# Eight-core two-layer block on Trainium2: two diagonal tiles and a later evacuation wait in the layer-0 convolution, one activation tile instead of two in the layer-1 QKV projection

## The chip, the cores and the metric

The kernel runs on the 8 cores of one Trainium2 chip, two dies of four cores. Every core runs the same program on its own batch element (2048 tokens of 1024 features). The time is device microseconds of the slowest core, from launch to end; lower is better. TensorE (PE) does matmuls, VectorE (DVE) and ScalarE (ACT) do elementwise work, GpSimd (POOL) issues the weight loads, and SyncE (SP) issues the other DMAs.

## The reference, cut to what matters

Two layers. Each is `x = x + s * g` with `s` an attention-like branch and `g` a silu-gated feed-forward branch on the layernormed input. The change touches one step of each layer's attention branch.

```
# layer 0: projection, causal depthwise convolution over 4 taps, then value and gate
z = x @ W_in
z = conv_general_dilated(z, w_conv, padding=[(CONV_K - 1, 0)], feature_group_count=...) + b_conv
x_val = z[..., :D]                  # 1024 channels
x_gate = silu(z[..., D:2 * D])      # 1024 channels
...                                 # decayed running sums, norm, W_out
# layer 1: projection to q, k, v
qkv = hidden_states @ Wqkv.T + bqkv
...                                 # rope, windowed attention, full attention, Wd
```

Layer 0's feed-forward works on fake-quantized operands; layer 1's is a mixture of 8 experts (MoE).

## The kernel before, in words

**Layer 0 attention** (`emit_l0_attn`) walks over 4 chunks `tc` of 512 tokens. In each chunk the first stage is the projection with the convolution, 16 feature blocks `fc`:

- POOL loads the block's weights (`wfc`, 256 KB) into one of two buffers, after the projection that used this buffer two blocks before.
- PE runs 8 matmuls of 512 columns into PSUM (L769).
- DVE copies 3 old columns (L773), casts the PSUM bank to the bf16 tile `zr` (L775), keeps the last 3 columns (L778), then builds four 128x128 diagonal matrices from the identity and the tap weights into the one tile `diag4` (L783), and signals with a small memset (L787).
- PE runs 4 matmuls, one for each tap, with the diagonals as stationary operand (L795).
- ACT evacuates that bank into `xv` (L799) or, with silu, into `gate` (L803).
- PE waits for ACT, and DVE for PE, before the next block.

After the 16 blocks comes DVE's scan for the denominator and its reciprocal (L827, L837), the main stage of the chunk, the output projection (L1053, with weight loads of the same size, L1044), and the residual (L1085). PE runs the first projection of the next chunk already during the residual.

**Layer 1 QKV** (`emit_l1_attn`) walks over 4 chunks `tt` of 512 tokens. It has 32 output blocks `oc` in each: POOL loads 256 KB of weights (`wstq`, two buffers, L1676), PE runs 8 matmuls (L1686), and ACT evacuates with the bias (L1702, L1711). For the last 8 blocks SP transposes the result (L1721). The chunk's activations, `xnb_q` (1 MB), lie in two buffers. The load of chunk `tt + 1` is issued on SP at the start of chunk `tt`, behind the transposes of chunk `tt - 1` (L1663).

Of the kernel before, what the change touches and what calls it, by code (L numbers as in the profile page):

```python
# [7 lines left out]
BF16 = mybir.dt.bfloat16  # L8
U32 = mybir.dt.uint32
AF = mybir.ActivationFunctionType  # L10
ALU = mybir.AluOpType
# [18 lines left out]
class KB:  # L30
# [75 lines left out]
    def wait(self, eng, sem, val):  # L106
        assert val <= self.cnt(sem), (sem, val, self.cnt(sem))
        self.q[eng].append(
            lambda E, _s=sem, _v=val: E[eng].wait_ge(E["S"][_s], _v))
# [549 lines left out]
def emit_l0_attn(kb, pb, want_dbg=False):  # L659
    H, op, wait, drain = kb.H, kb.op, kb.wait, kb.drain  # L660
    sb = kb.sb
# [4 lines left out]
    smalls = sb["smalls"]  # L666
# [8 lines left out]
    wre = kb.S("wre", (128, 32), F32)  # L675
    wim = kb.S("wim", (128, 32), F32)
    wy = kb.S("wy", (128, 8 * 128), BF16)
    diag4 = kb.S("diag4", (128, 4 * 128), BF16)
    zr = [kb.S(f"zr{i}", (128, TC + 3), BF16) for i in range(2)]
    ztail = kb.S("ztail", (128, 16 * 3), BF16)  # L680
    xv = kb.S("xv", (128, 8 * TC), F32)
# [69 lines left out]
    for tc in range(NTC):  # L751
        t0 = tc * TC
        first = tc == 0
        for fc in range(16):
            bz = fc % 2
            in_ap = bass.AP(H["l0_win2"].tensor, fc * 131072,
                            [[1024, 128], [1, 1024]])
            if wfc_guard[bz]:
                kb.wait("gpsimd", "te", wfc_guard[bz])
            lw = op("gpsimd", lambda e, _i=in_ap, _b=bz: e.dma_start(  # L760
                out=wfc[_b][:], in_=_i), "gw", 16)
            wait("tensor", "gw", lw)
            bank = pb[2 + bz]
            mmv = None
            for dc in range(8):
                mov = xn_fm[:, dc * T + t0:dc * T + t0 + TC]
                sta = wfc[bz][:, dc * 128:(dc + 1) * 128]
                mmv = op("tensor", lambda e, _b=bank, _s=sta, _m=mov, _d=dc:
                         e.matmul(_b[:], _s, _m, start=(_d == 0), stop=(_d == 7)),  # L769
                         "te" if dc == 7 else None)  # L770
            wfc_guard[bz] = mmv
            wait("vector", "te", mmv)
            op("vector", lambda e, _b=bz, _f=fc: e.tensor_copy(  # L773
                zr[_b][:, 0:3], ztail[:, _f * 3:_f * 3 + 3]))
            ev = op("vector", lambda e, _b=bank, _z=bz: e.tensor_copy(  # L775
                zr[_z][:, 3:3 + TC], _b[:]), "dve")
            kb.drain("vector")
            op("vector", lambda e, _b=bz, _f=fc: e.tensor_copy(  # L778
                ztail[:, _f * 3:_f * 3 + 3], zr[_b][:, TC:TC + 3]))
            wait("tensor", "dve", ev)  # L780
            wait("vector", "te", wfc_guard[bz])
            for tap in range(4):
                op("vector", lambda e, _f=fc, _t=tap: e.tensor_scalar(  # L783
                    out=diag4[:, _t * 128:(_t + 1) * 128], in0=sb["ident"][:],
                    scalar1=wconv[:, (_f * 4 + _t):(_f * 4 + _t) + 1],
                    scalar2=None, op0=ALU.mult))
            v_diag = op("vector", lambda e: e.memset(smalls[:, 3:4], 0.0), "dve")  # L787
            wait("tensor", "dve", v_diag)
            bank2 = pb[4 + bz]
            mmv2 = None  # L790
            for tap in range(4):
                mov = zr[bz][:, tap:tap + TC]
                sta = diag4[:, tap * 128:(tap + 1) * 128]
                mmv2 = op("tensor", lambda e, _b=bank2, _s=sta, _m=mov, _t=tap:
                          e.matmul(_b[:], _s, _m, start=(_t == 0), stop=(_t == 3)),  # L795
                          "te" if tap == 3 else None)
            wait("scalar", "te", mmv2)
            if fc < 8:
                a = op("scalar", lambda e, _b=bank2, _f=fc: e.activation(  # L799
                    xv[:, _f * TC:(_f + 1) * TC], _b[:], AF.Identity,  # L800
                    bias=bconv[:, _f:_f + 1], scale=1.0), "act")
            else:
                a = op("scalar", lambda e, _b=bank2, _f=fc: e.activation(  # L803
                    gate[:, (_f - 8) * TC:(_f - 7) * TC], _b[:], AF.Silu,
                    bias=bconv[:, _f:_f + 1], scale=1.0), "act")
            wait("tensor", "act", a)
            wait("vector", "te", mmv2)
        a_convdone = kb.cnt("act")

        if want_dbg and "dbg_xv" in H:  # L810
# [812 lines left out]
def emit_l1_attn(kb, want_dbg=False):  # L1623
# [13 lines left out]
    ones1b = sb["ones1b"]  # L1637
    relub, ubuf = sb["relub"], sb["ubuf"]
    M_R = kb.marker()
    xnb2 = [kb.S(f"xnb_q{i}", (128, 8 * 512), BF16) for i in range(2)]  # L1640
    wst = [kb.S(f"wstq{i}", (128, 8 * 128), BF16) for i in range(2)]
    rot = kb.S("rot", (128, 128), BF16)
    cosl = kb.S("cosl", (128, 512), BF16)
# [5 lines left out]
    wst_guard = [0, 0]  # L1649
    evac_hist = []  # L1650
    vtp_hist = []
    mm_tt = [0, 0]
    lx_t = {0: op("sync", lambda e: e.dma_start(
        out=xnb2[0][:], in_=bass.AP(H["xn1"].tensor, 0,
                                    [[2048, 128], [128 * 2048, 8], [1, 512]])),
        "ld", 16)}
    for tt in range(4):
        xnb = xnb2[tt % 2]
        if tt + 1 < 4:
            if mm_tt[(tt + 1) % 2]:  # L1660
                wait("sync", "te", mm_tt[(tt + 1) % 2])
            lx_t[tt + 1] = op("sync", lambda e, _t=tt + 1,
                              _o=xnb2[(tt + 1) % 2]: e.dma_start(  # L1663
                out=_o[:],
                in_=bass.AP(H["xn1"].tensor, _t * 512,
                            [[2048, 128], [128 * 2048, 8], [1, 512]])),
                "ld", 16)
        lx = lx_t[tt]
        wait("tensor", "ld", lx)
        for oc in range(32):  # L1670
            bws = oc % 2
            if wst_guard[bws]:
                kb.wait("gpsimd", "te", wst_guard[bws])
            in_w = bass.AP(H["l1_wqkvT"].tensor, oc * 131072,
                           [[1024, 128], [1, 1024]])
            lww = op("gpsimd", lambda e, _i=in_w, _b=bws: e.dma_start(  # L1676
                out=wst[_b][:], in_=_i), "gw", 16)
            wait("tensor", "gw", lww)
            if len(evac_hist) >= 4:
                wait("tensor", "act", evac_hist[-4])  # L1680
            bank = pb[oc % 4]
            mmv = None
            for dc in range(8):
                mmv = op("tensor", lambda e, _b=bank, _s=wst[bws][:, dc * 128:(dc + 1) * 128],
                         _m=xnb[:, dc * 512:(dc + 1) * 512], _d=dc:
                         e.matmul(_b, _s, _m, start=(_d == 0), stop=(_d == 7)),  # L1686
                         "te" if dc == 7 else None)
            wst_guard[bws] = mmv
            mm_tt[tt % 2] = mmv
            wait("scalar", "te", mmv)  # L1690
            if oc < 4:
                dst = qsl[:, oc * T + tt * 512:oc * T + tt * 512 + 512]
            elif oc < 8:
                dst = ksl[:, (oc - 4) * T + tt * 512:(oc - 4) * T + tt * 512 + 512]
            elif oc < 16:
                dst = qrest[:, (oc - 8) * T + tt * 512:(oc - 8) * T + tt * 512 + 512]
            elif oc < 24:
                dst = krest[:, (oc - 16) * T + tt * 512:(oc - 16) * T + tt * 512 + 512]
            else:
                dst = v_tm[:, (oc - 24) * T + tt * 512:(oc - 24) * T + tt * 512 + 512]  # L1700
            if oc < 24:
                a_e = op("scalar", lambda e, _b=bank, _d=dst, _o=oc: e.activation(  # L1702
                    _d, _b, AF.Identity, bias=sb["bqkv_t"][:, _o:_o + 1],
                    scale=1.0), "act")
                evac_hist.append(a_e)
            else:
                vstage = sb["relub"] if (oc % 2 == 0) else sb["ubuf"]
                if len(vtp_hist) >= 2:
                    wait("scalar", "tp", vtp_hist[-2])
                a_e = op("scalar", lambda e, _b=bank, _o=oc, _v=vstage:  # L1710
                         e.activation(_v[:], _b, AF.Identity,  # L1711
                                      bias=sb["bqkv_t"][:, _o:_o + 1],
                                      scale=1.0), "act")
                evac_hist.append(a_e)
                wait("sync", "act", a_e)
                pair = oc - 24
                sa = vstage[:].rearrange("p (i q) -> p i q", q=128)
                da = bass.AP(v_tm, pair * T + tt * 512,
                             [[8 * T, 128], [128, 4], [1, 128]])
                tpv = op("sync", lambda e, _s=sa, _d=da:  # L1720
                         e.dma_start_transpose(_d, _s), "tp", 16)  # L1721
                vtp_hist.append(tpv)
# [556 lines left out]
```

How the kernel before makes its waits and increments, by code:

```python
    def op(self, eng, f, inc=None, n=1):  # L89
        if inc is None:
            self.q[eng].append(lambda E, _f=f: _f(E[eng]))
            return None
        if n == 16:
            prev = self.counts.get(inc, 0)
            if prev:
                self.wait(eng, inc, prev)
        self.counts[inc] = self.counts.get(inc, 0) + n
        v = self.counts[inc]
        self.q[eng].append(
            lambda E, _f=f, _s=inc, _n=n: _f(E[eng]).then_inc(E["S"][_s], _n))
        return v
# [4 lines left out]
    def wait(self, eng, sem, val):  # L106
        assert val <= self.cnt(sem), (sem, val, self.cnt(sem))
        self.q[eng].append(
            lambda E, _s=sem, _v=val: E[eng].wait_ge(E["S"][_s], _v))
```

## Time and profile before

| | us |
|---|---|
| median of 3 runs | 6670.56 (6667.47 to 6677.14) |
| profiled execution, its own time | 6681.63 |
| its span, core 0, the slowest | 6680.3 |
| spans of the 8 cores | 6645.3 to 6680.3 |
| PE, DVE, ACT, POOL busy on core 0 | 2580.4, 2019.9, 1265.4, 189.0 |
| mean granted TensorE clock of the cores | 0.636 to 0.639 |

A time beside a line is the engine's busy time in that group. "Idle before" is how long the engine stood still just ahead of the group, with what released it. The releaser is inferred from semaphore events: where an instruction waits for several semaphores the view names only one. The granted clock is a share of 2.4 GHz: 512 columns take 0.213 us at 2.4 GHz and 0.427 us at 1.2 GHz. The time outside the span is 1.3 us.

### The profile page before, as it was taken

To read this page: it belongs to the slowest core of one execution; us is meant where nothing else is said; L and a number is where in the kernel's file an instruction comes from. 1 tells how busy PE (TensorE), PEld (TensorE's weight loads), DVE (VectorE), ACT (ScalarE), POOL (GpSimd) and SP (SyncE) were. 2 spreads that over 40 slices of the span, in tenths; PEclk is the share of its full clock that TensorE was granted. 3 is DMA by queue.
4 is the path that set the end of the run, shared out by engine and by line. 5 is a ranking of instruction groups with operands and counts; after the bars stand their busy time and mean duration, and the time that the engine had idled before them with its cause. 6 is when DMAs were issued, how large, how long until landed. Compare 5 with 4: busy or idle time off the path is not lost.

```text
span 6680.3 us, 35761 instructions; the slowest of 8 cores (6645.3 to 6680.3 us)
## 1 busy us (share of the span) xinstructions
PE 2580.4 (39%) x8358; PEld 826.1 (12%) x8358; DVE 2019.9 (30%) x4521; ACT 1265.4 (19%) x2230; POOL 189.0 (3%) x358
## 2 busy tenths in 40 slices
PE   0005422422423422105444555534444655555531
PEld 0002100100100100002111211101111311111110
DVE  8882463364365166121110000021222011111121
ACT  0001120110111021001110111104333244444300
POOL 0000000000000000000000011100000000000000
PEclk9997555655555555558777877755555855555576
DMA  2211102101200200434555444420000300000024
GB/s 51 47 42 15 18 0 46 23 0 27 42 0 12 56 2 1 91 67 77 72 82 76 85 66 68 62 33 1 1 1 1 51 2 5 5 5 5 8 51 134
DMA packets 271576, 239.39 MB, mean 36 GB/s; under 512 B 191826, under 2 KB 213970, under 8 KB 271346
## 3 DMA queue, kind: packets, MB, share of 16 engines
q0 software_dynamic: 52768, 116.50, 12.1%
q1 hardware_dynamic: 218610, 120.60, 8.8%
q8 instruction: 81, 1.33, 0.1%
q14 instruction: 117, 0.96, 0.1%
HBM read 284.17 MB, written 25.17 MB: 46 GB/s over the span
## 4 chain that ended last, share of the span: by engine, by line
DMA 30%; DVE 24%; PE 24%; ACT 10%; issue 9%; DVEq 2%; SPq 0%; ACTq 0%; POOLq 0%
DMA wstq<-l_wqkvT 8%; PE PS L2106 4%; ACT ptcol L2086 3%; PE PS L769 3%; DMA maskb<-masksf 3%; DVE csre L925 2%; DVE csim L928 2%; PE PS L2075 2%; DMA wst<-l_wd 2%; ACT ptw L1879 2%; DMA wgu<-l_wg 2%; DMA wgu<-l_wu 2%; PE PS L1999 2%; DMA wfc<-l_win 2%; DMA wfc<-l_wout 1%
## 5 line engine op out<-in xcount | busy, mean ns | idle before, releaser
L1686 PE MATMUL PS<-xnb_q,wstq 128*128 128x512 bf16 x1024 | 344.0, 497 | 281.8 <-DMA wstq<-l_wqkvT 255.7
L2086 ACT ACTIVATE ptcol<-PS,negmb 128x512 bf16<-128x512 f32 (+3 forms) x640 | 357.5, 623 | 469.0 <-PE PS L2075 468.9
L947 PE MATMUL PS<-rein,psum 128*32 128x512 bf16 x128 | 76.4, 597 | 869.8 <-DVE imin L941 869.8
L1551 PE MATMUL PS<-xnb,wgu 128*128 128x512 bf16 x1024 | 260.5, 420 | 321.2 <-DMA xnb<-xn 235.5
L2106 PE MATMUL PS<-ptcol,a 128*65 128x512 bf16 (+3 forms) x640 | 281.2, 556 | 237.6 <-ACT ptcol L2086 128.8
L2075 PE MATMUL PS<-xn_fm,g 64*128 64x512 bf16 (+3 forms) x640 | 277.1, 555 | 127.8 <-DMA A_fm<-outsb 127.3
L769 PE MATMUL PS<-xn_fm,wfc 128*128 128x512 bf16 x512 | 219.7, 606 | 97.8 <-DMA wfc<-l_win 61.1
L549 PE MATMUL PS<-xq_fm,wqT 128*128 128x512 bf16 x256 | 57.1, 387 | 495.5 <-DMA wqT<-wq_st 495.5
L891 ACT ACTIVATE sinb<-frac 128x512 bf16<-128x512 f32 x128 | 73.0, 617 | 874.9 <-DVE frac L884 874.9
L1742 DVE TENSOR_TENSOR qsl<-qsl,cosl 128x512 bf16<-128x512 bf16 x16 | 6.8, 426 | 716.8 <-DMA g<-ubuf 682.6
L1568 DVE TENSOR_TENSOR relub<-relub 128x512 bf16<-128x512 bf16 x64 | 27.2, 426 | 648.4 <-ACT ubuf L1563 648.4
L795 PE MATMUL PS<-zr,diag 128*128 128x512 bf16 x256 | 90.3, 489 | 271.1 <-DVE smalls L787 271.1
L1895 PE MATMUL PS<-g,ptw 128*128 128x64 bf16 x256 | 54.4, 212 | 340.2 <-DVE ptw L1884 340.2
L1686 PEld LDWEIGHTS PS<-xnb_q,wstq 128*128 128x128 bf16 x1024 | 110.9, 116 | 514.5 <-issue 466.0
L1597 PE MATMUL PS<-inter,wst 128*128 128x512 bf16 x512 | 140.5, 437 | 87.0 <-DMA wst<-l_wd 51.2
L2092 DVE TENSOR_TENSOR ptcol<-ptcol,cmask 128x128 bf16<-128x128 bf16 x256 | 57.7, 225 | 365.8 <-ACT ptcol L2086 365.8
L1551 PEld LDWEIGHTS PS<-xnb,wgu 128*128 128x128 bf16 x1024 | 106.5, 106 | 474.8 <-issue 380.6
L925 DVE TENSOR_TENSOR_SCAN csre<-rein,carr 128x512 bf16<-128x512 bf16 x128 | 162.6, 1271 | 7.0 <-DVE imin L919 0.5
L2063 DVE COPY a<-A_tm 128x64 bf16<-128x64 bf16 x256 | 46.1, 180 | 391.2 <-PE PS L2106 391.2
L928 DVE TENSOR_TENSOR_SCAN csim<-imin,carr 128x512 bf16<-128x512 bf16 x128 | 161.0, 1258 | 0.0
L1884 DVE TENSOR_TENSOR ptw<-ptw,wmask 128x256 bf16<-128x256 bf16 (+1 forms) x256 | 73.8, 288 | 263.4 <-ACT ptw L1879 263.4
L1920 ACT ACTIVATE A_tm<-PS,rdc 128x64 bf16<-128x64 f32 x256 | 80.4, 314 | 364.9 <-DVE rdc L1914 364.9
(268 smaller groups left out, 4194.5 us busy)
## 6 DMA issues: line engine op xcount, KB each, us to landing
wstq<-l_wqkvT POOLq DMA_DIRECT2D x128, 256.0 KB, 4.1
wfc<-l_win POOLq DMA_DIRECT2D x64, 256.0 KB, 3.9
wgu<-l_wg POOLq DMA_DIRECT2D x32, 512.0 KB, 5.2
wgu<-l_wu POOLq DMA_DIRECT2D x32, 512.0 KB, 5.2
wst<-l_wd POOLq DMA_DIRECT2D x32, 512.0 KB, 5.6
xt<-x SPq DMA_DIRECT2D x16, 512.0 KB
wfc<-l_wout POOLq DMA_DIRECT2D x32, 256.0 KB, 3.9
xt_l<-x SPq DMA_DIRECT2D x16, 512.0 KB
```

Source lines behind the costliest of these rows:

```text
L769: e.matmul(_b[:], _s, _m, start=(_d == 0), stop=(_d == 7)),
L795: e.matmul(_b[:], _s, _m, start=(_t == 0), stop=(_t == 3)),
L925: op("vector", lambda e, _ci=ci, _p=p: e.tensor_tensor_scan(csre[_p][:], rein[_p][:], rein[_p][:], carr[:, _ci:_ci + 1], ALU.add, ALU.bypass))
L928: g = op("vector", lambda e, _ci=ci, _p=p: e.tensor_tensor_scan(csim[_p][:], imin[_p][:], imin[_p][:], carr[:, _ci + 1:_ci + 2], ALU.add, ...
L1551: _h=hc: e.matmul(_b, _s, _m, start=(_h == 0), stop=(_h == 7)),
L1597: e.matmul(_b, _s, _m, start=(_k == 0), stop=(_k == 15)),
L1686: e.matmul(_b, _s, _m, start=(_d == 0), stop=(_d == 7)),
L1879: e.activation(ptw[_b][:, 0:_n], _S[:, 0:_n], AF.Exp, bias=negmb1[:, _h:_h + 1], scale=0.125),
L1999: _d=dc: e.matmul(_b, _s, _m, start=(_d == 0), stop=(_d == 7)),
L2075: _w=w, _r=half * 64: e.matmul(PS[:, _o:_o + _w], _k, _q, start=True, stop=True, tile_position=(_r, 0)), "te")
L2086: e.activation(ptcol[:, _o:_o + _w], PS[:, _o:_o + _w], AF.Exp, bias=negmb2[:, _h:_h + 1], scale=0.125), "act")
L2106: e.matmul(PS[0:65, OB0 + _q * 128:OB0 + _q * 128 + _w], a65[_b][:, 0:65], _p, start=_st, stop=_sp), "te")
```

## The change

It has two parts, in two stages that lie some 1500 us apart.

In the convolution `diag4` becomes two tiles. The diagonals of block `fc + 1` are built on DVE right after the copies of block `fc`, the first ones at the head of the chunk. The small memset is gone. PE no longer waits for ACT after each block. Its tap matmuls wait for the evacuation two blocks before, which used the same PSUM bank, and one wait for all evacuations stands behind the 16 blocks. DVE's wait for the tap matmuls is gone.

In the QKV projection the two tiles for the activations become one. The load of a chunk is issued at the chunk's head, when all matmuls before it are done.

```diff
-    diag4 = kb.S("diag4", (128, 4 * 128), BF16)
+    diag4 = [kb.S(f"diag4_{i}", (128, 4 * 128), BF16) for i in range(2)]
...
+        def build_diag(fcx):
+            for tap in range(4):
+                g = op("vector", lambda e, _f=fcx, _t=tap, _d=diag4[fcx % 2]:
+                       e.tensor_scalar(
+                    out=_d[:, _t * 128:(_t + 1) * 128], in0=sb["ident"][:],
+                    scalar1=wconv[:, (_f * 4 + _t):(_f * 4 + _t) + 1],
+                    scalar2=None, op0=ALU.mult), "dve" if tap == 3 else None)
+            return g
+
+        wait("vector", "te", kb.cnt("te"))
+        diag_v = {0: build_diag(0)}
+        act_hist = []
...
+            if fc + 1 < 16:
+                diag_v[fc + 1] = build_diag(fc + 1)
             wait("tensor", "dve", ev)
-            wait("vector", "te", wfc_guard[bz])
-            for tap in range(4):
-                op("vector", lambda e, _f=fc, _t=tap: e.tensor_scalar(
...
-            v_diag = op("vector", lambda e: e.memset(smalls[:, 3:4], 0.0), "dve")
-            wait("tensor", "dve", v_diag)
+            wait("tensor", "dve", diag_v[fc])
+            if len(act_hist) >= 2:
+                wait("tensor", "act", act_hist[-2])
...
-            wait("tensor", "act", a)
-            wait("vector", "te", mmv2)
+            act_hist.append(a)
+        wait("tensor", "act", kb.cnt("act"))
...
-    xnb2 = [kb.S(f"xnb_q{i}", (128, 8 * 512), BF16) for i in range(2)]
+    xnb = kb.S("xnb_q", (128, 8 * 512), BF16)
...
-            lx_t[tt + 1] = op("sync", lambda e, _t=tt + 1,
-                              _o=xnb2[(tt + 1) % 2]: e.dma_start(
...
+        wait("sync", "te", kb.cnt("te"))
+        lx = op("sync", lambda e, _t=tt: e.dma_start(
+            out=xnb[:], in_=bass.AP(H["xn1"].tensor, _t * 512,
                                     [[2048, 128], [128 * 2048, 8], [1, 512]])),
-        "ld", 16)}
```

PE, the first blocks of a chunk, before. PS is PSUM, `wfc` the projection weights, `diag` the diagonals.

```order
L769 MATMUL PS<-xn_fm,wfc 128x512 [waits act,gw]
L769 MATMUL PS<-xn_fm,wfc 128x512 x7
L795 MATMUL PS<-zr,diag 128x512 [waits dve]
L795 MATMUL PS<-zr,diag 128x512 x3
L769 MATMUL PS<-xn_fm,wfc 128x512 [waits act,gw]
L769 MATMUL PS<-xn_fm,wfc 128x512 x7
```

The same place now (L781 is the projection, L804 the taps).

```order
L781 MATMUL PS<-xn_fm,wfc 128x512 [waits gw]
L781 MATMUL PS<-xn_fm,wfc 128x512 x7
L804 MATMUL PS<-zr,diag_0 128x512 [waits dve,act]
L804 MATMUL PS<-zr,diag_0 128x512 x3
L781 MATMUL PS<-xn_fm,wfc 128x512 [waits gw]
L781 MATMUL PS<-xn_fm,wfc 128x512 x7
L804 MATMUL PS<-zr,diag_1 128x512 [waits dve,act]
```

The order of the matmuls is the same. The wait for ACT has moved from the projection to the taps, where it asks for an evacuation two blocks old.

DVE in the same blocks, before.

```order
L773 COPY zr<-ztail 128x3 [waits te]
L775 CAST zr<-PS 128x512
L778 COPY ztail<-zr 128x3
L783 TENSOR_SCALAR diag<-ident,wconv 128x128 [waits te]
L783 TENSOR_SCALAR diag<-ident,wconv 128x128 x3
L787 MEMSET smalls 128x1
```

And now (L757 builds diagonals, L787 is now the cast).

```order
L757 TENSOR_SCALAR diag_1<-ident,wconv 128x128 x4
L785 COPY zr<-ztail 128x3 [waits te]
L787 CAST zr<-PS 128x512
L790 COPY ztail<-zr 128x3
L757 TENSOR_SCALAR diag_0<-ident,wconv 128x128 x4
```

The diagonals that the taps of a block read now stand ahead of that block's copies.

SP in the QKV stage from its first instruction, before. `xnb_q` is the activation tile, `g` the transposed values.

```order
L1653 DMA xnb_q<-xn 128x8x512 [waits ld]
L1663 DMA xnb_q<-xn 128x8x512 [waits ld]
L1721 DMA_TRANSPOSE g<-relub 128x4x128 [waits act,tp]
...
L1721 DMA_TRANSPOSE g<-ubuf 128x4x128 [waits act,tp]
L1663 DMA xnb_q<-xn 128x8x512 [waits te,ld]
```

And now.

```order
L1663 DMA xnb_q<-xn 128x8x512 [waits te,ld]
L1718 DMA_TRANSPOSE g<-relub 128x4x128 [waits act,tp]
...
L1718 DMA_TRANSPOSE g<-ubuf 128x4x128 [waits act,tp]
L1663 DMA xnb_q<-xn 128x8x512 [waits te,ld]
```

One of the two loads at the head is gone. The load that stands behind the eight transposes of a chunk used to bring the chunk after next, and now brings the next one.

## Rows read from the trace of the kernel before

**Rows 1.** Costliest groups: line, engine, operation; busy us, mean ns; idle before, releaser.
```profile
L769 PE MATMUL PS<-xn_fm,wfc 128*128 128x512 bf16 x512 | 219.7, 606 | 97.8 <-DMA wfc<-l_win 61.1
```

**Rows 2.** Timeline of one block, first chunk: start, us, engine, line; idle before, releaser.
```profile
641.53 3.57 PE L769 MATMUL PS<-xn_fm,wfc 128*128 128x512 bf16 x8 [1.03 <-ACT xv L799]
...
645.29 0.69 DVE L775 CAST zr<-PS 128x512 bf16<-128x512 f32 x1
...
646.17 0.84 DVE L783 TENSOR_SCALAR diag<-ident,wconv 128x128 bf16<-128x128 bf16 x4
646.96 0.06 DVE L787 MEMSET smalls<- 128x1 f32 x1
...
647.17 1.02 PE L795 MATMUL PS<-zr,diag 128*128 128x512 bf16 x4 [2.06 <-DVE smalls L787]
648.29 0.69 ACT L799 ACTIVATE xv<-PS,bconv 128x512 f32<-128x512 f32 x1 [7.01 <-PE PS L795]
...
649.23 3.46 PE L769 MATMUL PS<-xn_fm,wfc 128*128 128x512 bf16 x8 [1.03 <-DMA wfc<-l_win]
```

**Rows 3.** Timeline of POOL, third and fourth weight load of the first chunk.
```profile
616.00 0.53 POOL L760 DMA_DIRECT2D wfc<-l_win  x1 [3.87 <-DMA wfc<-l_win]
637.28 0.53 POOL L760 DMA_DIRECT2D wfc<-l_win  x1 [20.74 <-PE PS L769]
```

**Rows 4.** Chain of waits, first tap matmuls of the second and third chunk.
```profile
1159.71 1.88 PE PS L795 x4
...
1688.02 1.88 PE PS L795 x4
```

**Rows 5.** Timeline, last tap matmuls of the second and third chunk.
```profile
1278.56 1.02 PE L795 MATMUL PS<-zr,diag 128*128 128x512 bf16 x4 [1.96 <-DVE smalls L787]
...
1809.39 1.87 PE L795 MATMUL PS<-zr,diag 128*128 128x512 bf16 x4 [1.96 <-DVE smalls L787]
```

**Rows 6.** Timeline of POOL in the first output projection, first load and the seventh.
```profile
1079.68 0.53 POOL L1044 DMA_DIRECT2D wfc<-l_wout  x1 [330.37 <-PE PS L1053]
...
1106.76 0.53 POOL L760 DMA_DIRECT2D wfc<-l_win  x1 [3.87 <-DMA wfc<-l_wout]
```

**Rows 7.** Windows: stretch, us, busy by engine (instructions), granted clock, DMA share, GB/s.
```profile
630.00:751.00 121.00, 73.97 (x184) 21.20 (x184) 24.40 (x122) 11.59 (x16) 7.96 (x15) 0.64 0.23 32
3795.00:4408.00 613.00, 344.10 (x1025) 111.00 (x1025) 0.00 (x0) 87.97 (x128) 67.44 (x127) 0.77 0.47 66
...
6430.00:6540.00 110.00, 60.36 (x242) 22.16 (x243) 12.75 (x30) 20.61 (x30) 3.18 (x6) 0.95 0.25 54
```

**Rows 8.** Timeline, one group of the last projection, 8 matmuls.
```profile
6449.94 1.89 PE L2201 MATMUL PS<-A_tm,wstd 128*128 128x512 bf16 x8 [1.63 <-DVE xn_fm L2219]
```

**Rows 9.** Chain of waits, behind the convolution of the second chunk.
```profile
1279.69 1.27 DVE l L827
```

**Rows 10.** Chain of waits at the start of the QKV stage.
```profile
3786.24 8.38 DMA xnb_q<-xn
3794.62 0.39 issue
```

**Rows 11.** Timeline of SP at the second and third border between QKV chunks.
```profile
4104.16 0.48 SPq L1663 DMA_DIRECT2D xnb_q<-xn  x1
...
4254.95 1.19 SPq L1721 DMA_TRANSPOSE g<-ubuf  x1
```

**Rows 12.** Chain of waits at the same borders, weight loads.
```profile
4104.48 8.16 DMA wstq<-l_wqkvT
...
4113.17 3.96 DMA wstq<-l_wqkvT
...
4262.39 3.82 DMA wstq<-l_wqkvT
```

**Rows 13.** Costliest groups, MoE.
```profile
L1551 PE MATMUL PS<-xnb,wgu 128*128 128x512 bf16 x1024 | 260.5, 420 | 321.2 <-DMA xnb<-xn 235.5
```

**Rows 14.** Chain of waits, the MoE load of the same tensor.
```profile
3232.47 6.70 DMA xnb<-xn
```

More of the change, by code:

```diff
@@ L779, in emit_l0_attn @@
                 ztail[:, _f * 3:_f * 3 + 3], zr[_b][:, TC:TC + 3]))
+            if fc + 1 < 16:
+                diag_v[fc + 1] = build_diag(fc + 1)
             wait("tensor", "dve", ev)
-            wait("vector", "te", wfc_guard[bz])
-            for tap in range(4):
-                op("vector", lambda e, _f=fc, _t=tap: e.tensor_scalar(
-                    out=diag4[:, _t * 128:(_t + 1) * 128], in0=sb["ident"][:],
-                    scalar1=wconv[:, (_f * 4 + _t):(_f * 4 + _t) + 1],
-                    scalar2=None, op0=ALU.mult))
-            v_diag = op("vector", lambda e: e.memset(smalls[:, 3:4], 0.0), "dve")
-            wait("tensor", "dve", v_diag)
+            wait("tensor", "dve", diag_v[fc])
+            if len(act_hist) >= 2:
+                wait("tensor", "act", act_hist[-2])
             bank2 = pb[4 + bz]
@@ L792, in emit_l0_attn @@
                 mov = zr[bz][:, tap:tap + TC]
-                sta = diag4[:, tap * 128:(tap + 1) * 128]
+                sta = diag4[fc % 2][:, tap * 128:(tap + 1) * 128]
                 mmv2 = op("tensor", lambda e, _b=bank2, _s=sta, _m=mov, _t=tap:
@@ L1651, in emit_l1_attn @@
     vtp_hist = []
-    mm_tt = [0, 0]
-    lx_t = {0: op("sync", lambda e: e.dma_start(
-        out=xnb2[0][:], in_=bass.AP(H["xn1"].tensor, 0,
+    for tt in range(4):
+        wait("sync", "te", kb.cnt("te"))
+        lx = op("sync", lambda e, _t=tt: e.dma_start(
+            out=xnb[:], in_=bass.AP(H["xn1"].tensor, _t * 512,
                                     [[2048, 128], [128 * 2048, 8], [1, 512]])),
-        "ld", 16)}
[L1657 to L1661, printed above, removed]
-            lx_t[tt + 1] = op("sync", lambda e, _t=tt + 1,
-                              _o=xnb2[(tt + 1) % 2]: e.dma_start(
[L1664 to L1668, printed above, removed]
+            "ld", 16)
         wait("tensor", "ld", lx)
@@ L1688, in emit_l1_attn @@
             wst_guard[bws] = mmv
-            mm_tt[tt % 2] = mmv
             wait("scalar", "te", mmv)
```

## The prediction

> **What bounds the kernel now.** I read the page's groups first. In the layer-0 projection PE stands idle 97.8 us ahead of its 512 matmuls, most of it put down to the weight DMA [rows 1]. That would mean that the convolution stage is bound by its loads, so I checked it in the timeline of one block [rows 2]. The reader is to see a closed ring there: projection on PE from 641.53 for 3.57, DVE's cast, four diagonals, the memset, the taps on PE at 647.17, ACT's evacuation at 648.29, and only then the next projection at 649.23. No two engines work side by side. The view names the DMA as what released 649.23. But the load that this fourth block needs is the fourth one, issued at 637.28 [rows 3], 12 us earlier, and the load before it had POOL waiting only 3.87 us for its predecessor. ACT ended at 648.29 + 0.69 = 648.98, and PE began 0.25 us later. So the ring is the bound, and the DMA in that row is the wrong name: the order lists show two waits there, for act and gw.
>
> How long the ring takes: the second chunk runs from its first taps at 1159.71 [rows 4] to its last at 1278.56 [rows 5], 118.85 us for 15 blocks, 7.92 each; the third from 1688.02 to 1809.39, 121.37 us, 8.09 each. The first and fourth lie between them. Four chunks at the mean of the two are 480.4 us, for 60 block periods of 8.01.
>
> The QKV stage is another case: at its borders POOL's weight loads follow one another in the chain of waits [rows 12], and PE waits for them. PE time there is not on the path; what shifts the weight loads is.
>
> **Part one, the convolution: what goes.** Three pieces leave the ring.
> - The diagonals and the memset. The taps begin when the cast is done, 645.29 + 0.69 = 645.98, plus the 0.15 us that the signal took from the memset's end, 647.02, to 647.17: 646.13 instead of 647.17, 1.04 us less. The four diagonals (0.84 us, the same four instructions as before) now run on DVE beside the taps and the next projection. All of DVE's work for a block, from the cast's start to the memset's end, is 647.02 - 645.29 = 1.7 us, against a period over 4: covered. Without cover it would be the 1.04 again.
> - The evacuation. The projection used to begin 2.06 us after the taps' start; now it follows four matmuls of 0.213 us, 0.85 us after it at the high clock: 1.2 us less. The new wait of the taps for the evacuation two blocks back asks for something a whole period old. Behind it stand only the taps and the next projection.
> - DVE's wait for the taps, which only matters at a chunk's end (below).
>
> **What is late next.** Two things can be. PE alone: projection 1.89 us at 2.4 GHz [rows 8] or 3.57 at 1.2 [rows 2], then 1.03 from its end to the taps (0.88 for the cast, 0.15 for the signal), then 0.85 for the taps, or 1.71 at 1.2 GHz. That is 3.77 us with all at the high clock, 5.45 with the projection alone at the low one, 6.31 with both. And the weight chain: POOL keeps one 256 KB load in flight. The output projection has loads of the same size, back to back: from 1079.68 to 1106.76 [rows 6], 27.08 us for 6, 4.51 each. So the period cannot fall much under 4.5 even when PE could do it in 3.77.
>
> Which clock? The stage was granted 0.64 with PE in ring waits half the time [rows 7]. In the last projection PE works 1.89 us and waits 1.63 [rows 8], and is granted 0.95. In QKV there are 128 groups of 8 matmuls in 613 us, 4.8 each with 2.7 of PE, and it is granted 0.77. The new pattern has 12 matmuls, 2.6 us, in 4.5, with the waits split in two: more work in a period than in the last projection (8 matmuls, 1.7 us, in 3.5). I take mostly the high clock, hence the weight chain as the bound, with about one period in ten at 5.45: 4.6 us. Bounds: 4.4 from below (the load at 616.00 came after 3.87 us of waiting for the one before it and POOL's own 0.53 [rows 3]), 6.31 from above.
>
> The sum: 480.4 - 60 x 4.6 = 204.4 us.
>
> **The chunk's ends.** DVE's scan started 1279.69 - 1278.56 = 1.13 us after the last taps began [rows 5, 9], and stands in the chain. It now starts behind the last cast and copy, about when the taps begin: 1 us less, 2 where the taps are slow, 4 times: 5. At a chunk's head the first diagonals stand ahead of the cast instead of behind it, the same work; the memset's step is worth nothing. DVE's new wait there is for PE work that it needed anyway. I put the ends at 5 us, between 2 and 8. Together part one gives 209.
>
> **Part two, the QKV projection: what comes.** At the first chunk nothing changes for PE: its load took 8.38 us and 0.39 to start [rows 10]. At three borders the load is now in the open. It is issued where the load for the chunk after next stood in SP's list, so at the second border at 4104.16, at the third after the last transpose, 4254.95 + 1.19 = 4256.2 with the queue's steps [rows 11]. It has one weight load beside it, like the first one, so 8.38 and 0.39: PE starts at 4112.9 and 4265.0. POOL's next weight load must wait for that group's end, at the low clock 3.57 later, and 0.6 for POOL: 4117.1 and 4269.2. Before, these loads were issued at 4113.17 and 4262.39 [rows 12]. The second border costs 3.9, the third 6.8. The second is cheap because the early load had its own price there: the weight load beside it took 8.16 us where its neighbour took 3.96. The first border had one too; I price it at the mean, 5.4. Part two costs 3 x 5.4 = 16 us. From below 11: with 6.70 us for the load, as in MoE [rows 14], each border is 1.7 cheaper. From above 26: 8.77 us at each of three, nothing given back.
>
> The Trainium skill (DMA: Bandwidth & Descriptors, Rules for kernel authors) says to issue a DMA early and wait for it late, which speaks against this part. By it alone the whole 8.77 us of each border is lost, 26 us, and the sum would be 10 us worse. Here the trace agrees in sign only.
>
> Net: 6681.63 - 209 + 16 = 6488.6 for the profiled execution. That one lay 11.07 above the median of 6670.56, so the median to expect is 6477.5; I say 6477.
>
> **Rivals.**
> - *A, the low clock stays.* PE splits its work by two waits in every period and is granted no more than now. Then the period is 5.45 rather than 4.6: 51 us less gain, 6528; at 6.31 it is 6580. For it: the stage had only 0.64, and QKV with waits of similar length 0.77 [rows 7]. Against it: the last projection at 0.95. The Trainium skill (TensorE: Matmul & The Clock Gate, A second HAM failure mode: psum-queue depth-cycling) describes this case: short idle spells between groups of matmuls that cycle through PSUM banks make the clock swing between its two levels. By it the time would be rival A's; the row of the last projection does not agree, the row of QKV does.
> - *B, the change does not open the ring.* If the row that names the DMA at 649.23 were right [rows 2], the next projection would need a load that is issued only after the last one, and the period would lose little: 0.4 us at most over 60 blocks, 24, less the 16 of part two, 6663. Against it: the count of loads above.
> - *C, slower.* The exposed load behaves like that in MoE, where PE waited 235.5 us over four chunks for the chunk's data, 58.9 each [rows 13]. There are no mask loads ahead of it here. Its place is each of three borders, and it decides from (209 + 13) / 3 = 74 us a border, where the time is 13 us above the present one. At 80 us a border it is 6702. At MoE's own 58.9 it would still be 6638.
>
> **How the numbers follow.** The forecast 0.64, with its own range: periods of 4.4 to 4.9 and part two from 11 to 26 give 6460 to 6505. Rival A 0.29, between 6505 and 6580. B 0.04, within 0.2% of the present time, which is 13 us and about what a measurement of this kernel can tell from no change. C 0.03. The range takes in most of A, and 20 us under the forecast's own low end, since all loads here that I could time stood beside other work: 6440 to 6560. Faster 0.93, same 0.04, slower 0.03.
>
> **What would show it.** In the changed trace the taps should begin about 1.0 us after the projection's last matmul, with no diagonal between cast and taps; the next projection 0.9 to 1.7 us after the taps' start when its weights are there; from the third block of a chunk on, PE waits for `wfc` truly, with POOL's loads 4.4 to 4.9 us apart. Fifteen blocks take 66 to 74 us instead of 119 to 121. The stage's granted clock is 0.85 or more; under 0.75 is rival A. In QKV three idle spells of PE, 10 to 13 us each, are put down to `xnb_q`, and no weight load takes 8 us. A stage of the kernel outside these two that moves by more than 10 us would be something I have not seen.

## The result and the profile after

The changed kernel takes 6435.88 us (median of 8 runs, 6430.25 to 6448.53), the kernel before 6670.71 us on the same chip (8 runs). The ratio is 0.9648 with the interval 0.9638 to 0.9659. That is 234.8 us less. The forecast was 193.6 less, and the time lies 4 us under the low end of the range.

The table gives means over the eight cores in the profiled executions. The first row runs from the first projection matmul to the last matmul of the output projection, the last one to the last matmul of all, and the other two from a stage's first matmul to the next stage's. "Load interval" is the median time from one weight load's issue to the next, taken for each core and then averaged.

| us | before | after | forecast |
|---|---|---|---|
| layer-0 projection to output projection, 4 chunks | 2086.0 | 1855.6 | -209 |
| MoE | 757.8 | 753.3 | 0 |
| QKV | 600.6 | 595.7 | +16 |
| rest of layer 1 | 2137.0 | 2136.7 | 0 |
| load interval, convolution stage | 7.60 | 4.36 | 4.6 |
| load interval, output projection | 4.52 | 4.34 | none |
| load interval, QKV | 4.62 | 4.42 | none |

The timeline of one block of the second chunk, on core 4, the slowest; the columns are start, us, engine, line, operation, and the idle time before with what ended it. It answers to [rows 2].

```profile
1139.02 1.89 PE L781 MATMUL PS<-xn_fm,wfc 128*128 128x512 bf16 x7
...
1141.09 0.69 DVE L787 CAST zr<-PS 128x512 bf16<-128x512 f32 x1
...
1141.94 0.74 DVE L757 TENSOR_SCALAR diag<-ident,wconv 128x128 bf16<-128x128 bf16 x4
...
1142.13 1.03 PE L804 MATMUL PS<-zr,diag 128*128 128x512 bf16 x4 [1.23 <-DVE zr L787]
1143.26 0.69 ACT L812 ACTIVATE gate<-PS,bconv 128x512 bf16<-128x512 f32 x1 [2.20 <-PE PS L804]
...
1143.44 1.89 PE L781 MATMUL PS<-xn_fm,wfc 128*128 128x512 bf16 x8 [0.28 <-DMA wfc<-l_win]
```

The ring is open. The diagonals run beside the taps, ACT evacuates beside the next projection, and PE waits for the cast and then, for 0.28 us, for its weights. Here the view's `wfc` is right: POOL's loads follow one another without slack, unlike those of [rows 3]. Its timeline in the first chunk:

```profile
649.24 0.53 POOL L772 DMA_DIRECT2D wfc<-l_win  x1 [3.72 <-DMA wfc<-l_win]
653.56 0.53 POOL L772 DMA_DIRECT2D wfc<-l_win  x1 [3.79 <-PE PS L804]
658.06 0.53 POOL L772 DMA_DIRECT2D wfc<-l_win  x1 [3.98 <-DMA wfc<-l_win]
662.32 0.53 POOL L772 DMA_DIRECT2D wfc<-l_win  x1 [3.73 <-PE PS L804]
```

These are 4.32, 4.50 and 4.26 us apart. Two of the rows name PE, and there the view has the wrong name once more: from the fifth block of a chunk on, 376 of the 384 loads of all cores are issued 0.53 us after the load before them has landed. The first and last taps and the scan of the second chunk, which answer to [rows 4, 5, 9]:

```profile
1103.21 1.87 PE L804 MATMUL PS<-zr,diag 128*128 128x512 bf16 x4 [45.37 <-DVE zr L787]
...
1168.26 1.27 DVE L836 TENSOR_TENSOR_SCAN l<-rp,carr 32x512 f32<-32x512 f32 x1
...
1168.45 1.03 PE L804 MATMUL PS<-zr,diag 128*128 128x512 bf16 x4 [1.23 <-DVE zr L787]
```

Fifteen blocks take 65.24 us instead of 118.85, 4.35 each. The scan begins 0.19 us before the last taps instead of 1.13 behind them. The windows, with [rows 7] to compare; behind the stretch come its length, the busy time of PE, PEld, DVE, ACT and POOL, the granted clock, the DMA share and GB/s:

```profile
631.00:695.00 64.00, 43.88 (x176) 16.25 (x178) 22.77 (x102) 11.59 (x16) 7.39 (x14) 0.97 0.39 55
1103.00:1168.00 65.00, 44.38 (x176) 16.53 (x180) 23.53 (x105) 11.59 (x16) 7.39 (x14) 0.95 0.40 59
```

PE is busy 68 to 69% of these stretches and is granted 0.95 to 0.97, against 0.64 before. Then QKV. The chain of waits at its start and its three borders, start and us, for [rows 10, 12]:

```profile
3549.26 8.09 DMA xnb_q<-xn
...
3705.16 6.69 DMA xnb_q<-xn
3711.85 0.49 issue
3712.35 3.59 PE PS L1684 x8
...
3857.45 6.72 DMA xnb_q<-xn
...
4007.16 7.30 DMA xnb_q<-xn
```

The activation load is now in the chain three more times, and the group behind it runs at the low clock (3.59 us). The page's costliest groups, for [rows 13] and QKV:

```profile
L1684 PE MATMUL PS<-xnb_q,wstq 128*128 128x512 bf16 x1003 | 335.5, 492 | 276.2 <-DMA wstq<-l_wqkvT 220.1
...
L1560 PE MATMUL PS<-xnb,wgu 128*128 128x512 bf16 x1003 | 263.5, 426 | 322.3 <-DMA xnb<-xn 235.6
...
wstq<-l_wqkvT POOLq DMA_DIRECT2D x128, 256.0 KB, 3.9
wfc<-l_win POOLq DMA_DIRECT2D x64, 256.0 KB, 3.8
```

MoE's wait for its activations is what it was (235.5). The last two lines give the median from issue to landing, and in the page of before the first of them is this:

```profile
wstq<-l_wqkvT POOLq DMA_DIRECT2D x128, 256.0 KB, 4.1
```

The same load of the same size lands 0.2 us sooner, though the change leaves it alone. That is what the forecast had not seen, and most experiments are about it.

### The profile page after: what moved, and what is told of

It reads as the page before. It is cut to its first block, busy times and chain, and to the rows that moved or that the text cites. A ratio compares the mean times of both kernels' runs of the same rounds, so it can differ in the third digit from the quotient of the medians.

```text
span 6428.9 us, 35465 instructions; the slowest of 8 cores (6416.6 to 6428.9 us)
## 1 busy us (share of the span) xinstructions
PE 2443.3 (38%) x8252; PEld 807.9 (13%) x8358; DVE 2016.7 (31%) x4457; ACT 1264.2 (20%) x2230; POOL 188.2 (3%) x358
## 4 chain that ended last, share of the span: by engine, by line
DMA 30%; DVE 25%; PE 22%; ACT 10%; issue 10%; DVEq 2%; SPq 1%; another core or an unknown queue 0%; ACTq 0%; POOLq 0%
DMA wstq<-l_wqkvT 6%; PE PS L2103 4%; ACT ptcol L2083 3%; DMA maskb<-masksf 3%; DVE csre L934 2%; DVE csim L937 2%; PE PS L2072 2%; DMA wst<-l_wd 2%; DMA wgu<-l_wg 2%; ACT ptw L1876 2%; DMA wgu<-l_wu 2%; PE PS L1996 2%; DMA wfc<-l_win 2%; DVEq L112 1%; PE PS L1560 1%
## 5 line engine op out<-in xcount | busy, mean ns | idle before, releaser
L804 PE MATMUL PS<-zr,diag 128*128 128x512 bf16 x251 | 68.2, 392 | 226.0 <-DVE zr L787 225.6
L1570 ACT ACTIVATE relub<-PS 128x512 bf16<-128x512 f32 x64 | 38.2, 597 | 550.8 <-PE PS L1560 490.4
```

## The experiments

Stage figures below are again means over the cores of one profiled execution each. Kernels given without a ratio were run once, and single times of one kernel lie up to 45 us apart (the kernel before, 25 runs: 6660.4 to 6705.4), so there the stage figures count and not the total.

**The two parts apart.** `conv_only` is the change without its QKV part, `qkv_only` is the kernel before with that part alone.

> The convolution part of the change alone; the QKV projection keeps its two activation tiles. The changed kernel gained 235 us where 193 was forecast. Its weight loads in QKV away from the borders between chunks follow one another every 4.46 us, before every 4.65 (means over the cores), and in the output projection every 4.4 instead of 4.5 to 4.7. Theory P (place): the load time depends on where the weight tile lies in SBUF, and QKV is quicker because its own tile has moved. Then QKV here stays at 4.65 and the kernel lies near 6670 - 232 = 6438. Theory T (traffic): the missing early load of 1 MB makes it quicker; same number here, 4.65. Theory C (carried over): the change in layer 0 leaves the cores in another phase to one another, which eases their loads; then QKV has 4.46 here too, without the border cost, and the kernel lies near 6415.

> The QKV part of the change alone; the convolution is that of before. Place and traffic: weight loads every 4.46 us between borders, 118 x 0.19 = 22 us less, three borders with 6 to 7 us more each, so no change: 6665 to 6672. Carried over: loads at 4.65 and the border cost in full, 6670 + 18 = 6688.

`conv_only` took 6412.93 us, ratio 0.9606 (0.9579 to 0.9632): 257 us less. `qkv_only` took 6690.71, ratio 1.0040 (1.0024 to 1.0056): 21 us more. On top of the convolution's change, part two costs 6435.9 - 6412.9 = 23. So the effects add up within the noise, and the surprise sits with the convolution's text: QKV takes 571.7 us in `conv_only`, where its code is that of before and took 600.6. From the load intervals I took the three around each border. They sum to 16.2, 15.7 and 14.5 us before, and to 21.8, 21.8 and 21.9 in `qkv_only`: 5.6, 6.1 and 7.4 more, 19 in all. Away from the borders the mean interval is 4.67 before, 4.57 in `qkv_only`, 4.45 in `conv_only` and 4.46 after. Over 118 intervals, 0.22 us are 26 of the 29 by which the stage is shorter in `conv_only`. In `qkv_only` the 0.10 takes 12 back, and in its profiled execution the stage is only 7 us longer than before (607.8); why the intervals are shorter there is not shown. The 21 us are those of the times, and the mean over the cores of the same runs gives 19 (6671.2 for 6652.4). In the page's row PE's busy and idle time for the stage fall from 344.0 + 281.8 us before to:

```profile
L1695 PE MATMUL PS<-xnb_q,wstq 128*128 128x512 bf16 x1024 | 331.2, 482 | 260.3 <-DMA wstq<-l_wqkvT 245.7
```

**Is it the place of the tiles in SBUF?** The smaller `xnb_q` moves the weight tiles by 8 KB. `qkv_pad` puts an unused tile there; `qkv_shift` keeps both tiles and moves the weights only.

```
qkv_pad:    xnb = kb.S("xnb_q", ...); pad_q = kb.S("pad_q", (128, 8 * 512), BF16)
qkv_shift:  xnb2 = [kb.S("xnb_q0", ...)]; wst = ...; xnb2.append(kb.S("xnb_q1", ...))
```

> As the QKV part alone (one activation tile, load exposed at each border), with an unused tile of 8 KB a partition behind the activation tile, so that the weight tiles lie where they lay before. Place: loads every 4.65 us, 6688. Traffic: 4.46 and 6668, like the run without the unused tile.

> The kernel before with its two activation tiles and early loads, but the second activation tile allocated behind the weight tiles, so that these lie where they lie in the changed kernel. Place: loads every 4.46 us between borders and no border cost, 6670 - 22 = 6648. Traffic: 4.65, 6670, no change.

`qkv_pad` 6690.51, ratio 1.0028 (1.0011 to 1.0045), as `qkv_only`; `qkv_shift` 6674.54, ratio 1.0000 (0.9985 to 1.0015), with QKV at 599.0. The place has nothing to do with it.

**The two halves of part one.** Both kernels have the QKV code of before. `diag_only` builds the diagonals early and keeps PE's wait for its own evacuation. `act_only` moves that wait two blocks back and keeps the diagonals between cast and taps.

```
diag_only:  part one, but   wait("tensor", "act", a); wait("vector", "te", mmv2)   kept
act_only:   part one, but   diag_v[fc] = build_diag(fc)   in block fc
```

> The convolution with the diagonals built a block ahead in two tiles, but PE again waits for ACT after every block and DVE for the taps; QKV is that of before. By the forecast's own step the ring loses 1.04 us a block at an unchanged clock: 60 x 1.04 = 62 us, 6608. If the shorter idle also lifts the clock (projection 1.89 instead of 3.57 us), the period is 1.89 + 1.03 + 2.06 = 5.0 instead of 8.0: 180 us, 6490. Whether QKV runs in 600 us (first matmul to the rotary stage, mean over the cores) as in the kernel before, or in 572 as with the whole convolution part, tells which piece of that part carries over.

> The convolution with the late wait for ACT and no wait of DVE for the taps, but the diagonals again built between cast and taps. At an unchanged clock 3.57 + 2.07 + 0.85 = 6.5 us a block instead of 8.0: 90 us, 6580. With the clock lifted 1.89 + 2.07 + 0.85 = 4.8: 192 us, 6478. QKV 600 or 572 us, as in the run with the diagonals alone.

`diag_only` 6540.69, ratio 0.9810 (0.9787 to 0.9833); `act_only` 6501.82, ratio 0.9752 (0.9731 to 0.9774). Both lie between their two expected values. PE's timeline in `diag_only`, and its window:

```profile
645.00 3.55 PE L781 MATMUL PS<-xn_fm,wfc 128*128 128x512 bf16 x8 [1.03 <-ACT xv L806]
649.67 1.02 PE L802 MATMUL PS<-zr,diag 128*128 128x512 bf16 x4 [1.12 <-DVE zr L787]
651.73 3.53 PE L781 MATMUL PS<-xn_fm,wfc 128*128 128x512 bf16 x8 [1.04 <-ACT xv L806]
```

```profile
631.00:695.00 64.00, 40.76 (x118) 12.80 (x120) 15.82 (x70) 8.12 (x11) 5.28 (x10) 0.78 0.25 37
```

And in `act_only`:

```profile
642.86 1.02 PE L802 MATMUL PS<-zr,diag 128*128 128x512 bf16 x4 [2.02 <-DVE diag L757]
643.72 1.89 PE L780 MATMUL PS<-xn_fm,wfc 128*128 128x512 bf16 x8
647.96 1.02 PE L802 MATMUL PS<-zr,diag 128*128 128x512 bf16 x4 [2.35 <-DVE diag L757]
648.82 3.44 PE L780 MATMUL PS<-xn_fm,wfc 128*128 128x512 bf16 x8
```

```profile
631.00:695.00 64.00, 42.28 (x129) 14.86 (x132) 16.28 (x74) 8.84 (x12) 5.29 (x10) 0.77 0.29 41
```

With one of the two waits left, part of the projections still run at 1.2 GHz and the stage is granted 0.77 to 0.78; only both edits together bring 0.95 and more. From the third block of a chunk on, counted on the six cores whose matmul records are complete, a projection takes over 2.2 us instead of 1.89 in all of 336 cases before, in 199 in `diag_only`, in 234 in `act_only` and in none in the changed kernel. In the layer-0 stage the halves save 103.7 and 131.8 us and the whole 230.4. The period in `diag_only` is 6.73 us, and 1.64 of that is the slower projection (3.53 for 1.89). So a good part of the whole change's gain is this clock, which the forecast had in its choice of period: by its own sum, 5.45 for 4.35 over 60 blocks would be 66 us. In both halves QKV is at 576 us.

**Two loads in flight.** If the weight chain bounds three stages, a second load beside the first must move all three. `two_loads` is `conv_only` with a semaphore for each buffer in the two projections of layer 0 and in QKV.

```
+ gs = "gx" if bz else "gw"
- out=wfc[_b][:], in_=_i), "gw", 16);  wait("tensor", "gw", lw)
+ out=wfc[_b][:], in_=_i), gs, 16);    wait("tensor", gs, lw)
```

> The convolution part alone, and POOL's weight loads of the layer-0 projection, the output projection and QKV on one semaphore for each buffer, so that two loads can be in flight. Theory of the load chain: each block there waits for one load at a time (4.35 us a block in the convolution, 4.37 in the output projection, 4.4 in QKV) and a load's time is mostly latency. Then the convolution falls to PE's own 3.98 a block (60 x 0.37 = 22 us), the output projection to about 3.0 (32 x 1.4 = 45 us), and QKV to 2.5 to 3.6 a block (128 x 0.8 to 1.9 = 100 to 240 us): 6413 - 22 - 45 - 100 to 240 = 6106 to 6246. Rival: the loads are bound by throughput shared with the other cores, two in flight take twice the time each, and nothing changes: 6413.

6270.49 us, ratio 0.9388 (0.9366 to 0.9409): the fastest version, 410 us under the kernel before on the same chip and 165 under the changed one's median on another. QKV falls to 465.7, the layer-0 stage to 1819.7. PE in its convolution stage, its window, and the page's QKV row:

```profile
642.02 1.02 PE L806 MATMUL PS<-zr,diag 128*128 128x512 bf16 x4 [1.23 <-DVE zr L789]
642.88 1.89 PE L783 MATMUL PS<-xn_fm,wfc 128*128 128x512 bf16 x8
646.00 1.02 PE L806 MATMUL PS<-zr,diag 128*128 128x512 bf16 x4 [1.23 <-DVE zr L789]
```

```profile
631.00:695.00 64.00, 41.86 (x179) 16.26 (x176) 27.86 (x105) 11.59 (x16) 7.93 (x15) 0.98 0.46 62
```

```profile
L1699 PE MATMUL PS<-xnb_q,wstq 128*128 128x512 bf16 x1024 | 281.2, 428 | 206.7 <-DMA wstq<-l_wqkvT 182.9
```

Now PE never waits for `wfc` in this stretch and the period is 3.98 us. So the load chain had been what set the 4.35. From first to last taps the four chunks take 250.0 us instead of the 261.8 of `conv_only`, the output projection 105.9 instead of 128.1, and QKV 106 us less: 12, 22 and 106, where 22, 45 and 100 to 240 were expected. In QKV a block takes 3.64 us on average instead of 4.47, not half. One reason is that two loads in flight land a little later (4.2 us instead of 3.9 in the pages, 4.0 instead of 3.8 over all cores). The larger one is in the chain of waits, here on core 5:

```profile
3801.68 3.90 DMA wstq<-l_wqkvT
3805.58 0.24 issue
3805.82 2.45 PE PS L1699 x8
...
3808.86 4.97 DMA wstq<-l_wqkvT
```

There are two weight buffers, and the load for a buffer is issued only when the matmuls that read it are done. Of the 1024 loads on all cores the view puts 990 down to PE, where in `conv_only` on its slowest core 125 of 128 are put down to the load before. Load, matmuls and the steps between them are 3808.86 - 3801.68 = 7.18 us here for two blocks. So the bound is now a ring through both buffers. Whether a third buffer would open it, no run shows.

**Is it the time at which the stages start?** `delay_conv` and `delay_before` put 16 memsets and a barrier in front of QKV, in `conv_only` and in the kernel before; the stage starts some 270 us later.

```
+ for _ in range(16): op("vector", lambda e: e.memset(kb.sb["A_tm"][:], 0.0), "dve"); kb.drain("vector")
+ kb.barrier()
```

> The convolution part alone with about 230 us of memsets on DVE and a barrier put in front of QKV, so that QKV starts as late as in the kernel before. If QKV is quicker there for its time of start or the cores' phase to one another, the interval of its weight loads changes from 4.4 us towards 4.65 (QKV from 572 towards 600). If it hangs on something that lasts from the convolution onwards, whatever the time, it stays at 572.

> The kernel before with the same memsets and barrier in front of QKV. Time of start or phase: QKV changes from 600 us. Something lasting: it stays at 600.

QKV 576.6 in the one, 594.8 in the other (totals 6683.85 and 6937.69, with the delay). The time of start is not it.

**Is it the memset, or the tile?** `no_memset` lets the last diagonal signal, `two_tiles` alternates between two tiles in the closed ring, `memset_back` is `conv_only` with a memset in each block.

```
no_memset:    ... scalar2=None, op0=ALU.mult), "dve" if tap == 3 else None);  v_diag = kb.cnt("dve")
two_tiles:    ... out=_d[:, ...] with _d=diag4[bz]
memset_back:  + op("vector", lambda e: e.memset(smalls[:, 3:4], 0.0))
```

> The kernel before, without the 64 small memsets: the fourth diagonal gives the signal. The ring loses some 0.05 us a block, 3 us, 6668. What it is for: all four kernels with a changed convolution ran their QKV weight loads every 4.37 to 4.42 us (medians over the cores), the four with the old one every 4.51 to 4.62, and a shift of QKV by 270 us changed neither. If the missing instructions are what lasts, 4.4 here and QKV in 572 to 577 us; if it is the broken ring itself, 4.6 and 600.

> The kernel before with two diagonal tiles used in turn, all waits and the order as before: no change in layer 0, 6670. If the 1 KB that all later tiles of layer 0 are shifted by is what makes loads quicker, the output projection's weight loads follow every 4.37 to 4.4 us instead of 4.57, and QKV's every 4.4; if not, 4.57 and 4.6.

> The convolution part alone with the 64 small memsets put back behind the diagonals, where DVE has time: no change in layer 0, 6413 in all. If the number of instructions is what lasts, QKV goes back to 600 us; if the open ring, it stays at 572.

QKV 595.3, 599.6 and 579.0; totals 6674.90, 6665.46 and 6412.72. Neither the memset alone nor the tile alone.

**Does an open ring leave something behind?** `open_first` opens the ring in chunk 0 alone, `open_last` in chunk 3 alone, and `chain_before` is the kernel before with 64 more weight loads one behind another ahead of QKV.

```
open_first:    closed = tc > 0;   if closed: wait("tensor", "act", a); wait("vector", "te", mmv2)
open_last:     closed = tc < 3
chain_before:  + for k in range(64): op("gpsimd", ... dma_start(out=wst[k % 2][:], ...), "gw", 16)
```

> The ring is open in chunk 0 alone, chunks 1 to 3 have one diagonal tile and the memset of before. All theories: the convolution stage is about 57 us shorter than before in chunk 0 only. Theory 'lasting': an open chunk leaves the cores in an order to one another that later loads inherit; QKV 572 to 580 us, total about 6585 us. Theory 'just before': what counts is how the cores come out of the last chunk; QKV 596 to 601 us as before, total about 6610 us.

> The ring is open in chunk 3 alone. Convolution about 57 us shorter there. Theory 'just before': QKV 572 to 580 us, total about 6585 us, and the interval of the output projection's loads falls to 4.4 us in chunk 3 alone. Theory 'needs the whole stretch': QKV 590 to 601 us, total about 6605 us.

> The kernel before with 64 additional 256 KB weight loads one behind another, then a barrier, in front of the QKV stage; the ring stays closed. Theory 'any load-bound stretch does it': QKV itself 572 to 580 us. Theory 'it takes the open ring': QKV 595 to 601 us. The additional loads cost 64 times 4.4 to 4.6 us, about 285 us, under either theory.

QKV 573.8, 575.4 and 597.4; totals 6595.91, 6570.50 and 6957.16. That looked like "lasting", but one figure did not fit. In `open_last` the output projection's load interval was 4.36 and 4.41 us in chunks 1 and 2, ahead of the only open chunk (before: 4.49 and 4.52). So the last question was whether the ring matters at all. `open_never` is the text of `open_first` with `closed = True`.

> The text of open_first with the ring closed in all four chunks (two diagonal tiles, no memset, the waits for the evacuation two blocks back and for the block's own evacuation). Convolution as before, 8.0 us a block less at most 0.1 for the memset. Theory 'it takes an open chunk somewhere': output projection 4.5 to 4.6 us a load, QKV 596 to 601 us, total 6660 to 6672 us. Theory 'a property of the program as compiled': output projection 4.35 to 4.42, QKV 572 to 580 us, total 6635 to 6645 us.

6638.04 us (the kernel before took 6710.30 in its one run beside it), with the convolution as slow as before (load interval 7.84 us, before 7.60; stage 2088.6 against 2086.0) and QKV at 578.3. Output projection: 4.36 to 4.43 in all four chunks. The theory of the open ring has fallen. Even the convolution's own loads, with the ring closed around them in both kernels, land a little sooner. The pages of `open_never` and then of the kernel before have:

```profile
wfc<-l_win POOLq DMA_DIRECT2D x64, 256.0 KB, 3.8
```

```profile
wfc<-l_win POOLq DMA_DIRECT2D x64, 256.0 KB, 3.9
```

Over all cores it is 3.87 us for 3.96, a smaller difference than the 0.2 us in QKV.

**Which edit?** `tiles_no_memset` has the two tiles and no memset, `waits_only` has the new waits beside the old ones.

```
waits_only:  - wait("vector", "te", wfc_guard[bz])
             + if len(act_hist) >= 2: wait("tensor", "act", act_hist[-2])
             + wait("vector", "te", kb.cnt("te"))     at the chunk's head
```

> The kernel before with two diagonal tiles and without the memset, its waits as before, ring closed. Convolution as before. Theory 'tiles and memset together': QKV 572 to 580 us, total 6635 to 6645 us. Theory 'the waits': QKV 595 to 601 us, total 6660 to 6675 us.

> The kernel before with its one tile and the memset, and with the new waits beside the old ones (PE for the evacuation two blocks back, DVE without its second wait for the projection), ring closed. Convolution as before. Theory 'the waits': QKV 572 to 580 us, total 6635 to 6645 us. Theory 'tiles and memset together': QKV 595 to 601 us, total 6660 to 6675 us.

QKV 600.5 and 598.6; totals 6675.01 and 6703.32, with 6665.65 for the kernel before beside them. Neither. `waits_only` came out 28 us over its expected range at the least; no part of that is in QKV.

Sixteen kernels have the double-buffered QKV code of before. Eight have the stage at 572 to 579 us: `conv_only`, `diag_only`, `act_only`, `delay_conv`, `memset_back`, `open_first`, `open_last`, `open_never`. Eight have it at 595 to 601: before, `qkv_shift`, `delay_before`, `no_memset`, `two_tiles`, `tiles_no_memset`, `waits_only`, `chain_before`. None lies between, and on four of the six chips used kernels of both kinds ran side by side. The first eight all have the function `build_diag` with two tiles and at least one of the changed waits, so it goes with the program's text, and `open_never` shows that no open ring is needed.

The traces hold a simpler mark. DVE's list, with all its semaphore and drain instructions, is 8001 to 8069 instructions long in the first eight kernels and 8129 to 8226 in the second. The two runs on the memset moved it by 64 each, from 8193 to 8129 and from 8005 to 8069, and so stayed on their side of the gap. The length of that list therefore fits all sixteen, and the memset runs do not exclude it. It is not shown to be the cause: no run changes the length and nothing else. The time itself is lost inside the transfer: from the first to the last of a QKV load's 128 packets of 2 KB it takes 2.24 to 2.30 us in the first eight and 2.38 to 2.42 in the second (medians over all cores), with 0.17 us for one packet in both. By what mechanism the program reaches the DMA stays open.

## Why the prediction was right and wrong

- **What bounds the stage: right.** The view named the DMA and the count of loads said the ring. Opening it took 8.01 - 4.35 = 3.66 us off a period; rival B would have left it at about 8.
- **The edits' own sizes: nearly right.** The gap from the projection to the taps was forecast as 1.03 and is 1.23 us: 0.15 was taken for the signal, from the memset's row, and behind the cast it is 1142.13 - 1141.78 = 0.35. The next projection was to begin 0.85 after the taps and does so in `two_loads`, 0.86. PE alone therefore needs 3.98, not 3.77. In the changed kernel the loads hide this.
- **The clock: right.** Expected 0.85 or more, measured 0.95 to 0.97. Rival A is out. The forecast still gave it 0.29, and took one period in ten at 5.45. On the six cores with complete matmul records 24 periods of 360 took 5.2 to 6.4 us, the one at each chunk's head, and none behind it did. The Trainium skill's rule (TensorE: Matmul & The Clock Gate, A second HAM failure mode: psum-queue depth-cycling), which would have given rival A, is not borne out by this stage, which was granted 0.95 to 0.97.
- **The weight chain as the next bound: right in kind, mis-sized.** This is one half of the step that failed, the time of a weight load. "4.51 each", from the output projection's rows [rows 6], was taken for the load and rounded up to 4.6 for low clocks, with 4.4 as the bound from below. Measured 4.35. That is 60 x 0.25 = 15 us, and it is the loads: the long periods came about as often as they were priced, and the other 336 took 4.21 on average.
- **Stages outside: wrong.** This is the other half, and the larger one: the forecast took a load's time for fixed and put every other stage that waits for loads at nothing, without a reason. The same 0.2 us a load was gained where the change does nothing: 118 intervals x 0.21 = 25 us in QKV, 20 x 0.2 = 4 in the output projection, 4.5 in MoE. The forecast held those at zero, and named a shift over 10 us outside as something it had not seen. It came inside the QKV stage, hidden under part two. Without these 33 us the time would have lain inside the range. What made the loads quicker stays open; the runs show that it needs neither the open ring nor part two.
- **The chunk's ends: right.** The scan begins 0.19 us before the last taps, 1.3 us earlier than before, for a forecast of 1.
- **Part two: right in kind, a little low.** Forecast 16 with bounds 11 and 26; measured 21 and 23 by the times and 19 by the load intervals. The loads took 6.69, 6.72 and 7.30 instead of 8.38, but the early load's price at the borders before, given back, was smaller than assumed (2.2, 1.7 and 0.5 us, the three intervals of [rows 12]'s borders against 3 x 4.67), so the second border cost 6.1 and not 3.9. The Trainium skill's rule (DMA: Bandwidth & Descriptors, Rules for kernel authors) to issue early and wait late is borne out in sign and, with 19 to 23 of the 26 us that the forecast worked out by it, nearly in size.

What the forecast missed adds up: 15 in the period, 4 in the output projection, 25 in QKV, 4.5 in MoE, less 3 to 7 for part two, is 42 to 46 against the 41 by which 6436 lies under 6477.

## What to carry to other kernels

When a view names a DMA behind a wait for two semaphores, count which load the instruction needs and when it was issued, and only then decide what the bound is. Where a chain of loads bounds a stage, its interval carries the forecast: some 0.2 us a load over 198 loads (60, 20 and 118) is the 40 us by which this one missed, most of them in stages that the change does not touch, so the range needs room there. And where one load at a time is the bound, a second semaphore for the second buffer is worth trying; here it brought another 142 us (6412.9 to 6270.5, on two chips), and what bounds QKV then is the number of buffers. When runs exclude an edit as a cause, ask whether they also exclude what it adds up to with others, here the length of an engine's list.

## What the runs showed of the hardware

- Weight loads of 256 KB, the same code and the same tiles, take 4.37 to 4.43 us from issue to issue in eight programs and 4.57 to 4.63 in eight others in QKV, and 4.32 to 4.45 against 4.51 to 4.57 in the output projection. Place in SBUF, start time, the 64 memsets alone, a second tile alone, the new waits alone and the open ring are excluded by runs. The length of DVE's list, 8001 to 8069 against 8129 to 8226 instructions, goes with it and is untested; the cause is not known.
- With two such loads in flight a QKV block takes 3.64 us against 4.47 with one: a gain of 19%, with the landing of each 0.2 to 0.3 us later. The ring of load, matmuls and next load through two buffers bounds it then, 7.2 us for two blocks in the rows above.
- The granted clock rose from 0.64 to 0.78 or 0.77 when one of two waits in a block was shortened, and to 0.95 and more with both. The two halves' gains in this stage, 104 and 132 us, add up to about the whole, 230.
